# Second graph layer of a four-layer network: the next block's selector products ahead of the look-up, and VectorE makes the parts of the first two blocks

## The reference

```
a_src = (h * att_src[None]).sum(-1)
a_dst = (h * att_dst[None]).sum(-1)
alpha = a_src[src] + a_dst[dst] + a_edge
alpha = jax.nn.leaky_relu(alpha, NEG_SLOPE)
amax = jax.lax.stop_gradient(jax.ops.segment_max(alpha, dst, num_segments=n))
ex = jnp.exp(alpha - amax[dst])
denom = jax.ops.segment_sum(ex, dst, num_segments=n)
att = ex / (denom[dst] + 1e-16)
msg = h[src] * att[:, :, None]
out = jax.ops.segment_sum(msg, dst, num_segments=n).reshape(n, H * C) + bias
```

## Time and profile before

| what | value |
|---|---|
| median of 3 runs | 2855.82 us (2853.89 to 2858.64) |
| profiled execution, its own time | 2853.28 us |
| profiled execution, span | 2851.1 us |
| mean granted TensorE clock | 0.92 of 2.4 GHz |
| first gather to the last sum of the stage | 888.9 to 1299.9 us |
| PE, DVE, ACT, POOL busy over the whole span | 84%, 55%, 29%, 21% |

### The profile page before, as it was taken

How to read it: one execution, slowest core, us unless ns; L and a number is a source line. 1 busy time by engine, 2 the same in 40 slices (tenths; PEclk the granted TensorE clock), 3 DMA queues, 4 the chain that set the end, 5 groups by cost and what they waited for, 6 DMA issues and landing times. The chain is left out here.

```text
span 2851.1 us, 31019 instructions
## 1 busy us (share of the span) xinstructions
PE 2391.1 (84%) x10568; PEld 1518.1 (53%) x10568; DVE 1580.6 (55%) x3570; ACT 830.1 (29%) x1868; POOL 610.6 (21%) x661
## 2 busy tenths in 40 slices
PE   3899957999964888885587999999999889959886
PEld 1356436999952666663453455444554434435443
DVE  9999554233443666776226999546983463531100
ACT  0156001111111677772112466114650200011010
POOL 0000533465403455540110000000000101012212
PEclk9999977999987899997598999999999899979998
DMA  4000554978834566761534544213531541359995
GB/s 138 1 1 20 156 151 145 308 247 273 291 99 143 165 186 187 202 160 47 178 117 170 194 169 156 91 64 123 195 120 38 182 142 43 133 199 381 372 355 196
DMA packets 169899, 466.00 MB, mean 163 GB/s; under 512 B 26365, under 2 KB 59117, under 8 KB 163888
## 3 DMA queue, kind: packets, MB, share of 16 engines
q1 hardware_dynamic: 124880, 357.25, 36.7%
q0 software_dynamic: 37808, 94.23, 12.4%
q10 hardware_dynamic: 7056, 12.55, 1.2%
HBM read 407.29 MB, written 56.44 MB: 163 GB/s over the span
## 5 line engine op out<-in xcount | busy, mean ns | idle before, releaser
L2280 PE MATMUL psum<-x_res,HH 125*128 125x512 f32 (+1 forms) x960 | 347.6, 521 | 10.2 <-DVE x_res L2484 9.3
L2280 PEld LDWEIGHTS psum<-x_res,HH 125*128 125x128 f32 x960 | 179.3, 191 | 167.9 <-issue 139.5
L849 POOL DMA_INDIRECT recd<-edge_records,edge_slots x160 | 193.2, 1208 | 247.2 <-issue 216.3
L1785 ACT ACTIVATE hg<-hg,ex 128x129 f32<-128x129 f32 x784 | 235.1, 388 | 1.6
L1619 POOL DMA_INDIRECT hg<-HT,srcidx x196 | 189.5, 967 | 133.3 <-POOLq L80 71.0
L2270 PE MATMUL psum<-W,XO 128*125 128x512 f32 x480 | 210.4, 600 | 0.0
L1743 PE MATMUL psum<-hg,Dh 128*125 128x258 f32 x784 | 196.9, 407 | 6.5 <-issue 4.3
L1233 PE MATMUL psum<-xgT,w 128*128 128x187 f32 x1024 | 173.0, 329 | 4.4 <-DMA w<-in_L_ffn_w 4.3
L1743 PEld LDWEIGHTS psum<-hg,Dh 128*125 128x125 f32 x784 | 152.6, 200 | 35.9 <-issue 8.4
L1233 PEld LDWEIGHTS psum<-xgT,w 128*128 128x128 f32 x1024 | 166.5, 194 | 9.0 <-DMA w<-in_L_ffn_w 5.6
L1242 PE MATMUL psum<-sums_room,w 128*128 128x187 f32 x1024 | 166.1, 322 | 0.0
(11 more groups left out here) (566 smaller groups left out, 3986.9 us busy)
## 6 DMA issues: line engine op xcount, KB each, us to landing
w<-in_L_ffn_w SPq DMA_DIRECT2D x64, 1024.0 KB
wd<-in_L_ffn_W_down SPq DMA_DIRECT2D x24, 2560.0 KB
MK<-CT SPq DMA_DIRECT2D x80, 625.0 KB
wu<-in_L_ffn_W_up SPq DMA_DIRECT2D x8, 2730.0 KB
wd_ahead<-in_L_ffn_W_down SPq DMA_DIRECT2D x6, 2560.0 KB
rows<-ROWS POOLq DMA_DIRECT2D x24, 625.0 KB, 6.7
DH<-hot ACTq DMA_DIRECT2D x49, 250.0 KB
Dh<-DH SPq DMA_DIRECT2D x49, 250.0 KB
```

Of the source, the lines that this page charges most:

```text
L849: g.nc.gpsimd.indirect_dma_start(out=g.recd, out_offset=bass.IndirectOffsetOnAxis(ap=g.posi[:, c:c + 1], axis=0), in_=g.E8[:, c, :], in_of ...
L1785: ins = act.activation(heads[:, h, :], heads[:, h, :], ACT.Copy, scale=ex[j % 2][:, c, h:h + 1])
L2280: return pe.matmul(flat[:, at:at + x1 - x0], HH[:, k, h * DH + c * 128:h * DH + c * 128 + 128], z[n % 4][:, x0:x1], start=(k == 0 and i < ...
```

## The change

Three edits, all in `gnn1_blocks`:

1. In TensorE's loop the spread of j+1 stands ahead of the look-up of j, for j from 1 on. For block 0 the look-up stands ahead of the turn and the spread of block 1.
2. `EASE = 2`: the parts and edge terms of blocks 0 and 1 are made by VectorE (`dve_parts`): those of block 0 ahead of its loop, those of block 1 behind the new maximum of block 0. GpSimd issues the gathers of four blocks without anything between, and then waits once for VectorE's parts (`rows`, `terms`) so that the counts of the two semaphores stay in order.
3. 20 matmuls of `keep_clock` ahead of the first turn.

```diff
-    HW, N4, RING, RH = NH * (DH + 1), CH * NH, 6, 4
+    HW, N4, RING, RH, EASE = NH * (DH + 1), CH * NH, 6, 4, 2
...
-            if j >= 2:
+            if j == EASE + 2:
+                pool.wait_ge(*rows.at(EASE))
+                pool.wait_ge(*terms.at(EASE))
+            if j >= EASE + 2:
                 pool_parts(j - 2)
-            if j >= 3:
+            if j >= EASE + 3:
                 pool_slot_terms(j - 3)
...
+    def dve_parts(j):
+        dve.wait_ge(*rows_in(j))
+        dve.tensor_copy(own_parts[j][:], hg[j][:, :, HW + NH:HW + NH + 6]).then_inc(*rows.up())
+        dve.tensor_tensor(q[j][:], hg[j][:, :, HW:HW + NH], rec(j)[:, :, 2:6], ALU.add).then_inc(*terms.up())
...
         dve_onehots(0)
+        dve_parts(0)
...
             dve_new_max(j, tiles[j])
+            if j + 1 < EASE:
+                dve_parts(j + 1)
...
         pe.wait_ge(*selected.at(1))
+        keep_clock(g, g.PS[:, 5, 128:BLK], 20)
         pe_turn(0)
         pe_spread(0)
+        pe_look_up(0)
         pe_turn(1)
+        pe_spread(1)
         for j in range(NB):
-            pe_look_up(j)
-            if j + 1 < NB:
+            if j and j + 1 < NB:
                 pe_spread(j + 1)
+            if j:
+                pe_look_up(j)
             if j + 2 < NB:
                 pe_turn(j + 2)
             if j:
```

## The result

| | before | after |
|---|---|---|
| median of 14 runs | 2857.11 us (2853.89 to 2872.54) | 2871.01 us (2858.35 to 2882.22) |
| profiled execution, own time and span | 2853.28, 2851.1 us | 2858.35, 2856.6 us |
| mean granted clock | 0.920 | 0.912 |

The ratio is 1.0041, with a 95% interval of 1.0025 to 1.0057: the change makes the kernel slower by 0.4%. The forecast was 2816 us. The profiled execution of after is its fastest of the 14, so the two traces differ by 5 us where the medians differ by 14.

The account below looks back on a forecast made before the run. A chain of waits, chiefly largest waiting for the spread's late news under gathers, was taken to set the pace; -36.1 + 1.2 - 5 = -39.9 from 2853.28 gave 2813.4, with the median 2.54 above: 2816 us, range 2788 to 2868.

Parts of the forecast that it names:

- The wait for the additions: VectorE's alpha under gathers: bound by the sums' additions, not the look-up, leaving 0.5 us of slack.
- The look-up's news is not [late]: TensorE's look-up to VectorE's alpha: its signal stays prompt under gathers, alpha following at 975.13 in the slow block too.
- rival B: Loop, chance 0.18: lateness moves to the look-up, so alpha waits; 0.45 to 0.6 us more per block, 2877 us.
- the fast block's phase: Loop under gathers: the spread starts at 1140.44, just ahead of the burst's first gather at 1140.76, and costs nothing.
- The period of 6.9: Loop: 6.9 us per block instead of 7.76, allowing one block in six at 8; saves 36.1 us over 42 blocks.
- The floor of 6.68: Loop under gathers: a block can't go below the fast block's 6.68 us, so at most 45.4 us is gained.
- the 12 us that I let come back: Loop: of largest's 57.2 us of removed wait, 12 return as the wait for the additions.
- The half microsecond of slack for alpha: VectorE's alpha under gathers: a look-up 0.24 us later hides behind 0.5 us of slack from the additions.
- The order's own cost in a quiet block: Blocks without gathers: 6.43 us against 6.18, costing 0.25 each, about 1.2 us over the last five.
- The opening: Stage's first blocks: VectorE making the early parts changes the time by -5 us, between +3 and -20.
- The clock: TensorE in the stretch: fewer idle gaps lift the mean clock from 0.93 to above 0.97; no separate term.
- the sign that the forecast gave for B: VectorE's alpha: waiting for the look-up by a us or more per block would show rival B.

Follow-up runs that it names:

- before, spread passed on by SyncE: Kernel before, the spread's signal to largest delayed on purpose through a small SyncE DMA: 2940.95 us in late conditions.
- before, look-up passed on: Kernel before, the look-up's signal to alpha delayed on purpose through a small SyncE DMA: 2920.22 us in late conditions.
- changed, spread passed on: Changed kernel, the spread's signal to largest delayed on purpose through a small SyncE DMA: 2876.95 us in late conditions.
- changed, look-up passed on: Changed kernel, the look-up's signal to alpha delayed on purpose through a small SyncE DMA: 2953.46 us in late conditions.
- the opening alone: Changed kernel with TensorE's loop order as before, keeping VectorE's parts and keep_clock: 2776.80 us, ratio 0.9983, in prompt conditions.
- the same opening with a tied burst: Old TensorE order with the opening's edits, GpSimd's burst for j (from 6) waiting for the look-up of j-4: 2776.45 us, ratio 0.9996.
- The tied bursts: GpSimd's bursts made to wait for TensorE's spread (changed kernel: 2779.90, again 2775.66 us) or look-up (kernel before: 2780.41; changed: 2777.01).

## Why the prediction was wrong

**What held.** Largest's wait was 57.2 us of news that came late, and the order removed it: 6.2 are left. The wait for the additions behind which alpha was to stand is short (9.2 us over the loop).

**The step that failed** is "The look-up's news is not [late]", with the reason given for it, that the look-up ends before the burst has begun to move much. The reason was wrong for the kernel before already. Of its 42 look-ups 12 end 1.6 to 4.8 us behind the first gather of their burst, and alpha follows within 0.04 in all 12, while the spread behind them is late in 11. One of them, timeline of before, 981 to 988 us:

```profile
981.85 0.98 POOL L1619 DMA_INDIRECT hg<-HT,srcidx  x1 [0.42 <-issue]
...
983.39 1.24 PE L1732 MATMUL psum<-AM,DT 125*128 x8 [2.65 <-DVE AM L1664]
...
984.42 1.92 PE L1722 MATMUL psum<-qT,sel 112*125 112x128 bf16 x16
984.67 0.17 DVE L1673 TENSOR_TENSOR al<-q,psum 128x16 f32<-128x16 f32 x1 [0.25 <-PE psum L1732]
...
987.68 0.69 DVE L1653 CUSTOM_DVE_ANT_0 junk<-mb,psum 125x512 f32<-125x512 bf16 x1 [1.77 <-PE psum L1722]
```

The look-up ends 2.78 behind the first gather and alpha starts 0.04 later; the spread ends 1.71 later still, and largest waits another 1.34. So the place in the burst isn't what kept the look-up's news prompt. What goes with it in the traces is the place on TensorE, ahead of the spread. Six traces are from late conditions. Of the look-ups that end 1.28 to 5.3 us behind the first gather, this many are prompt, that is, whoever waits for the signal (alpha; SyncE where it passes the look-up's news on) starts within 0.1 of their end:

| kernel | order | prompt |
|---|---|---|
| before | look-up first | 12 of 12 |
| before, spread passed on by SyncE | look-up first | 23 of 24 |
| before, look-up passed on | look-up first | 34 of 34 |
| changed | spread first | 0 of 16 |
| changed, spread passed on | spread first | 0 of 16 (one is 0.2 late, the others 1.5 to 5.0) |
| changed, look-up passed on | spread first | 0 of 20 |

The traces also record the semaphores' updates, with some missing. By these the spread ahead of the 16 look-ups of the changed kernel was itself 0.4 to 6.1 us late, in all 16. In the block shown above the spread is done at 1143.39; its signal goes through at 1149.27, the look-up's at 1149.36, the turn's at 1149.40.

That is rival B, with its place right (alpha), its price too high and its point wrong: I let it decide from a look-up's start 0.5 behind the first gather, but starts at 0.19 to 0.22 already fail in the changed kernel, and starts up to 2.8 behind it pass in the kernel before. Within the trace of after the place does matter. Look-ups that end up to 1.16 behind the first gather go through within 0.1; of those that end 1.28 to 1.32 behind it, seven, all come 6.27 to 6.48 behind that gather; two that end 1.7 and 1.9 behind it come at 4.3, and seven that end 3.8 to 5.2 behind it at 5.8 to 5.9. One ends 0.02 ahead of a burst's gathers and comes 6.1 behind them. The rest, which end at 5.9 or more, are prompt again.

The new order also drives the look-up to that edge. With both spread and turn done early, a block lasts 6.2 us, while GpSimd, when it needn't wait for the sum, starts the next burst after 5.55 (1137.55 to 1143.10 above). The burst gains 0.7 on the look-up per block until the look-up falls behind the edge, and the block takes 11 to 12 us; 15 of the 42 have alpha over 1 us late. I read the fast block's phase as one that would stay.

**The terms.** The period of 6.9 was to save 36.1 us; it was 7.99 and cost 9.6. The floor of 6.68, taken from the earlier trace rows, is none: blocks of 6.17 to 6.25 are in the trace of after, and 6.24 is the rule where news is prompt. So the wait of the additions was itself late news (of the sum, whose recorded signal is 0.6 to 1.3 us late in 20 blocks of the kernel before), and the 12 us that I let come back would not have. The half microsecond of slack for alpha isn't there either: a look-up made late is paid in full. The order's own cost in a quiet block was put at 0.25 and is 0.04, which is why the changed kernel equals the one before in prompt conditions. The opening was put at -5 and is +0.9 by the fourth block (alpha waited 12.6 us for the first look-up again). In prompt conditions it gives 0.4 by the fourth block (36.3 against 36.8). A ratio of 0.9983 for the opening alone is more than that explains, and the same opening with a tied burst gave 0.9996, so I don't count it.

The clock was to rise above 0.97 and fell to 0.88. It is lower where the loop has longer waits: 1.00 where news is prompt, 0.93 before, 0.88 after, 0.63 with 10 us of delay per block. B's price, 0.45 to 0.6 per block, was too high; 0.23 was paid, with 18 of the 42 blocks below 7 us. Alpha's wait of 76.9 us, 1.8 per block, is the sign that the forecast gave for B.

**The rule that spoke against the reading.** The forecast weighed the Trainium skill, "SBUF - State Buffer", section "Who interferes with whom": PE and ACT never wait on anyone, and DMA never contends with a compute engine. By that the lateness would be TensorE's own, and the forecast took from it that it would travel to whatever stands behind the spread. That consequence is what the traces show. The signal is late for three receivers alike, though the sum starts on time behind the turn. But TensorE isn't free of it: in seven blocks its sum stands still in parts of the burst with no semaphore to wait for, and no row says what holds it. The rule is on access to the buffer and says nothing of signals, so it doesn't settle which of the two is held, work or news.

**What stays open.** What makes news late in some groups and not in others, whether it is GpSimd's issuing or the gathers' traffic, and whether the signal itself or the last of TensorE's results is held, is not shown: ends of matmuls are modelled. Why spreads are held and look-ups ahead of them are not is open too; the stage's first look-up was held 11.4 us although it stood ahead of the next spread. The order without the opening was never run where news is late: in the table above the new order always comes with the opening's edits, which touch the first blocks alone. The tied bursts, which were to keep look-up and turn ahead of the edge, were never run there either, and are argued only. The best version in prompt conditions is the changed kernel with a burst that waits for the spread, with 0.9986 in one group and 1.0001 in the other: no gain that I would claim.

## What to carry to other kernels

When a wait ends late although the work behind the signal seems done, look at what stands ahead of that signal on its engine, and not only at the moment it falls in. In this loop the look-up was prompt at almost any point of the burst while it stood ahead of the spread, and late behind it: a swap can hand the lateness to the signal that had none. Before a swap, then, collect the blocks in which the prompt signal lies as deep in the burst as the late one. They were in the trace of before. A phase that drifts (here 0.7 us per block between two engines' loops) makes a rare long block out of a margin that looks safe in the blocks one has read. And run the kernel before again beside each experiment: here the 75 us between two sets of conditions were five times the effect that was to be explained.

## What the runs showed of the hardware

- In two groups of runs TensorE's semaphore signals, ready while four indirect gathers were issued, reached VectorE, ScalarE and SyncE up to 6.5 us behind the first gather; in the loops of four other groups, the kernel before and the changed one among them, within 0.1 us, with look-ups ending 0.3 to 6.8 behind the first gather.
- Where signals were late, a look-up's signal ready 1.28 to 5.3 us behind the first gather reached the engine that waited within 0.1 us in 69 of 70 cases when the look-up stood ahead of the spread on TensorE, and in 0 of 52 behind it (three traces each).
- In the seven blocks of the changed kernel with alpha about 5 us late, matmuls of TensorE's sum started up to 1.5 us apart with no semaphore to wait for, and it took 5.6 to 7.3 us in place of 3.75.
- VectorE's signals weren't so: in the kernel before the look-up started 0.25 us behind the new maximum in the median, and only 2 of 42 came over 0.5 later than that.
- The first four gathers of the stage could be used 10.3 us after the first was issued where news was late, and 10.1 where it was prompt (892.22 - 881.89, and 895.56 - 885.42).
- Cutting the rows of a gather from 2104 to 64 bytes left a gather's time on GpSimd, 0.96 us in the mean with either, and the pace of the loop as they were.
